# Selective-scan mixer: three of a state's four turned tiles weighed by ScalarE and summed in DRAM, one by VectorE

## The chip, the cores and the metric

One core of one Trainium2 chip runs the kernel. The metric is the device time of one execution in microseconds, the median over the runs; each run is one launch of the whole program.

## What is computed

The reference is a two-layer model on an input of 8 sequences of 512 tokens with 256 features. The change touches only the first mixer, a selective state-space scan with 512 channels and 16 states per channel, on each of the 8 sequences:

```
xz = x @ W_in;  xs, res = split(xz)
u = silu(grouped_conv4(xs) + conv_b)
dbc = u @ W_x                       # 64 columns for delta, 16 for B, 16 for C
delta = clip(softplus(dbc[:64] @ W_dt + b_dt), 0.001, 0.1)
dA = exp(delta * A)                 # per channel and state
h_t = dA_t * h_{t-1} + delta_t * u_t * B_t
y_t = sum over the 16 states n of h_t[n] * C_t[n]
out = (y + u * D) * silu(res) @ W_out
```

After it come an attention layer, a mixture of experts with routing, a second mixer and a second mixture of experts. All is float32.

## The kernel before

The program runs five stages one after the other; each ends with a barrier over the five engines. The first, StageA, is this mixer. Everything below is in it.

**States as the unit of work.** The work is cut into K = 128 states: 8 sequences (blocks b) times 16 states n, k = 16 b + n. A state has two halves f = 0 and 1 of 256 channels each (two groups of 128 partitions, 512 tokens along the free axis). For one half:

- `fill` (L695): GpSimd multiplies du = delta * u by the row of B of that state, which SP has broadcast from DRAM to all partitions (L383, 256 KB), into a buffer h (L702). There are eight such buffers, four states' worth.
- `drive` (L577): ScalarE writes the decays exp(delta * A) with two activations (L584) into PSUM, banks 0 and 1 for one half, 2 and 3 for the other.
- `recur` (L648): VectorE runs the recurrence over the tokens, in place in h (L652).
- `turn` (L465 on TensorE, L588 on ScalarE, L654 on VectorE): the product with C is a weight per token, so TensorE first turns h from channels-by-tokens into four tiles i = 0 to 3 of 128 tokens by 512 channels, four transposes each (L472). Bank 4 takes tiles 0 and 1, one after the other; VectorE multiplies each by its column of C and adds it to the running sum `acc` in SBUF (L665, or L662 without the add for the first state of a block). Bank 5 takes tiles 2 and 3; ScalarE multiplies each by its column into `pr` in SBUF (L599; for the first state straight into `acc`).
- `add` (L705): GpSimd issues a DMA that adds the two tiles of `pr` (512 KB) onto the half of `acc` that belongs to tiles 2 and 3 (L713). It waits for the DMA of the state before. There are two `pr` buffers.

**The order.** `order` (L318) writes one list of steps, and every engine walks it and does what concerns it, in that order. The list runs over half-states h = 2k + f. Within one, lines L333 to L344 decide:

```python
out += [step for step in pieces if step[0] in self.TAKE]
if k in range(K):
    out.append(("recur", k, f))
if f and k - 2 in range(K):
    out.append(("add", k - 2))
if k - 1 in range(K):
    out.append(("turn", k - 1, f))
if k + 1 in range(1, K):
    out.append(("drive", k + 1, f))
if k + 2 in range(1, K):
    out.append(("fill", k + 2, f))
out += [step for step in pieces if step[0] not in self.TAKE]
```

So a turn follows its scan by a state, an add by two, and a fill comes two states before its scan.

**The pieces.** What prepares the next block (layer norm, transposes, the projections and the convolution on TensorE, their evictions by ScalarE, the two Silus with their table loads, softplus, clip, du) and what finishes the block before (`back`, the sums turned back; `gate` on VectorE; `proj`, the output projection; `back_to_x`) is cut into pieces. Two tables written by hand, PREP (L295) and END (L309), deal them out over the 32 half-states of a block. PREP's numbers count from the start of the block before, END's from the start of the block after. `bank` (L278) hands PSUM banks 6 and 7 to the pieces in turn. The pieces of ScalarE that come closest together are `silu` (L551: a table load, two activations of 2048 columns, a table load) at half-state 16, `mixed` at 18, four `stepped` at 20 to 23, and `soft` (L573) at 23.

**Queues.** SP issues the broadcasts of B, each once GpSimd is through with the buffer two states back. GpSimd issues the adds between its own multiplications. `back` waits for all adds of its block (L478).

Of the kernel before, what the change touches and what calls it, by code (L numbers as in the profile page):

```python
# [219 lines left out]
class StageA:  # L220
# [6 lines left out]
    def __init__(self, m):  # L227
        self.m = m
        ar = Arena(m.Z, m.LO, m.HI)
# [8 lines left out]
        self.nb = ar.take([4])  # L238
        self.n_tm = ar.take([4, 256])
        self.n_fm = ar.take([2, 515])  # L240
        self.dbc = ar.take([512], parts=96)
        self.ct = [ar.take([4, 32]) for _ in range(2)]
# [11 lines left out]
        self.turn_d, self.turn_a = m.banks[4], m.banks[5]  # L254
        self.scr = [m.nc.dram_tensor(f"rows_b{q}", [16, 512], F32, kind="Internal").ap() for q in range(2)]
        self.steps = self.order()
        first = {}
        for what, *at in self.steps:
# [8 lines left out]
            "d_win", "d_conv", "d_rest", "d_scr", "pads", "neg", "win_t", "tapped", "taps", "moments", "rstd", "nb", "n_tm", "made0", "made1", "gate", "u",  # L267
            "raw", "delta", "du", "hin", "decay", "scan", "turn_d", "turn_a", "ysum", "yprod", "yadd", "yp")}

# [19 lines left out]
    def over(self, *step):  # L289
# [5 lines left out]
    PREP = (  # L295
        (-11, ("stats",)), (-10, ("rstd",), ("minus",)), (-9, ("norm",)), (-6, ("flip", 0)),
        (-5, ("flipped", 0), ("flip", 1)), (-4, ("flipped", 1)), (-3, ("conv", 0, 0), ("conv", 0, 1)),
        (-2, ("conv", 0, 2), ("conv", 0, 3)), (-1, ("conv", 0, 4)), (0, ("conv", 0, 5), ("conv", 0, 6)),
        (1, ("conv", 0, 7), ("conv", 1, 0)), (2, ("conved", 0), ("conv", 1, 1)), (3, ("conv", 1, 2), ("conv", 1, 3)),
        (4, ("conv", 1, 4), ("conv", 1, 5)), (5, ("conv", 1, 6)), (6, ("conv", 1, 7), ("conv", 2, 0)),  # L300
        (7, ("conved", 1), ("conv", 2, 1), ("conv", 2, 2)), (8, ("conv", 2, 3)), (9, ("conv", 2, 4), ("conv", 2, 5)),
        (10, ("conv", 2, 6), ("conv", 2, 7)), (11, ("conved", 2), ("conv", 3, 0)), (12, ("conv", 3, 1), ("conv", 3, 2)),
        (13, ("conv", 3, 3), ("conv", 3, 4)), (14, ("conv", 3, 5)), (15, ("conv", 3, 6), ("conv", 3, 7)),
        (16, ("conved", 3), ("silu",)), (17, ("mix",)), (18, ("mixed",)), (19, ("side",), ("step", 0)),
        (20, ("spill",), ("sided",), ("stepped", 0), ("step", 1), ("lift", 0)),
        (21, ("stepped", 1), ("step", 2), ("lifted", 0), ("lift", 1)), (22, ("stepped", 2), ("step", 3), ("lifted", 1)),
        (23, ("stepped", 3), ("soft",)), (24, ("clip",), ("lift", 2)), (25, ("du",), ("lifted", 2)), (26, ("lift", 3)),
        (27, ("lifted", 3)))
    END = (  # L309
        (7, ("back", 0)), (8, ("gate", 0), ("back", 1)), (9, ("gate", 1), ("back", 2)), (10, ("gate", 2), ("back", 3)),  # L310
        (11, ("gate", 3)), (12, ("proj", 0, 0), ("proj", 0, 1), ("proj", 0, 2)),
        (13, ("proj", 0, 3), ("proj", 0, 4), ("proj", 0, 5)), (14, ("proj", 0, 6), ("proj", 0, 7)), (15, ("back_to_x", 0)),
        (16, ("proj", 1, 0), ("proj", 1, 1), ("proj", 1, 2)), (17, ("proj", 1, 3), ("proj", 1, 4), ("proj", 1, 5)),
        (18, ("proj", 1, 6), ("proj", 1, 7)), (19, ("back_to_x", 1)))

    FIRST, LAST = -3, 16
# [37 lines left out]
    def sp(self, e):  # L354
# [29 lines left out]

        self.walk(spill=spill, fill=fill)

    def pe(self, e):
# [77 lines left out]
        def turn(k, f):  # L465
            for (o, i, free, made) in ((self.turn_d, f, "ysum", "turn_d"), (self.turn_a, 2 + f, "yprod", "turn_a")):
                if f == 0:
                    e.wait_ge(s["scan"], 2 * k + 2)
                if k or f:
                    e.wait_ge(s[free], 2 * k + f)  # L470
                for c in range(4):
                    ins = e.transpose(o[:, c * 128:(c + 1) * 128], self.h(k, c // 2)[:, c % 2, i * 128:(i + 1) * 128], ident)  # L472
                ins.then_inc(s[made], 1)

        def back(b, c):
            if c == 0:
                e.wait_ge(s["ysum"], 32 * (b + 1))
                e.wait_ge(s["yadd"], 16 * 15 * (b + 1))  # L478
            o = bank("back", b, c)
            for i in range(4):  # L480
                ins = e.transpose(o[:, i * 128:(i + 1) * 128], self.acc[b % 2][:, i, c * 128:(c + 1) * 128], ident)
            ins.then_inc(s["made1"], 1)
# [15 lines left out]
    def act(self, e):  # L498
# [26 lines left out]
        def norm(b):  # L525
            s6, mv, r = self.sb
            e.wait_ge(s["nb"], b + 1)
            if b:
                e.wait_ge(*self.made("flip", b - 1, 1))
            for i in range(4):  # L530
# [69 lines left out]

# [4 lines left out]
    def dve(self, e):  # L605
# [31 lines left out]
        def sided(b):  # L637
            o, over, before = self.bank("side", b)
            e.wait_ge(*self.made("side", b))
            if b >= 2:  # L640
                e.wait_ge(s["yprod"], 32 * (b - 1))
            e.tensor_copy(self.ct[b % 2].rearrange(FLAT), o[:, 0:128]).then_inc(*over)
# [10 lines left out]

        def turn(k, f):  # L654
            b, n = divmod(k, 16)
            e.wait_ge(s["turn_d"], 2 * k + f + 1)
            o, c = self.acc[b % 2][:, f, :], self.ct[b % 2][:, f, 16 + n:17 + n]
            if n == 0:
                e.wait_ge(*self.over("side", b))
                if b >= 2:  # L660
                    e.wait_ge(*self.made("back", b - 2, 3))
                e.tensor_scalar(o, self.turn_d, c, None, ALU.mult).then_inc(s["ysum"], 1)  # L662
            else:
                e.wait_ge(s["ysum"], 2 * (k - 1) + f + 1)
                e.scalar_tensor_tensor(o, self.turn_d, c, o, ALU.mult, ALU.add).then_inc(s["ysum"], 1)  # L665

# [19 lines left out]
    def pool(self, e):  # L686
# [8 lines left out]
        def fill(k, f):  # L695
            b, n = divmod(k, 16)
            if k % 16 == 0:
                e.wait_ge(s["du"], b + 1)
            e.wait_ge(self.d_B[k % 2], 16 * (k // 2 + 1))
            if k >= 4:  # L700
                e.wait_ge(s["turn_a"], 2 * (k - 4) + 2)
# [12 lines left out]

# [1802 lines left out]
```

## Time and profile before

| | us |
|---|---|
| median of 3 runs | 3337.27 |
| lowest and highest | 3325.84 and 3342.91 |
| the profiled execution, its own time | 3336.9 |
| its span, first to last instruction | 3335.1 |
| mean granted TensorE clock over it | 0.927 of full speed |
| first scan starts | 99.3 |
| last scan starts | 1001.1 |

The profile is of one execution. Engines: PE is TensorE, DVE VectorE, ACT ScalarE, POOL GpSimd. Busy time is that of instructions; an instruction that issues a DMA is not counted as busy. The idle time of a group is that of its engine just before it, with what ended it behind the arrow. Two instructions that follow each other on one engine can overlap by some 0.1 us in the trace, so the cost of one in a full stretch is best read from the distance of starts.

### The profile page before, as it was taken

To read this page: it belongs to the slowest core of one execution; us is meant where nothing else is said; L and a number is where in the kernel's file an instruction comes from. 1 tells how busy PE (TensorE), PEld (TensorE's weight loads), DVE (VectorE), ACT (ScalarE), POOL (GpSimd) and SP (SyncE) were. 2 spreads that over 40 slices of the span, in tenths; PEclk is the share of its full clock that TensorE was granted. 3 is DMA by queue.
4 is the path that set the end of the run, shared out by engine and by line. 5 is a ranking of instruction groups with operands and counts; after the bars stand their busy time and mean duration, and the time that the engine had idled before them with its cause. 6 is when DMAs were issued, how large, how long until landed. Compare 5 with 4: busy or idle time off the path is not lost.

```text
span 3335.1 us, 40739 instructions
## 1 busy us (share of the span) xinstructions
PE 2797.5 (84%) x13719; PEld 1686.9 (51%) x13782; DVE 2184.5 (65%) x3943; ACT 1569.1 (47%) x2311; POOL 1043.2 (31%) x705
## 2 busy tenths in 40 slices
PE   7778887787764699999966999948988887999999
PEld 3444454454452355555543666624444444666666
DVE  0698898899893676777532222226777775777776
ACT  2677667766761245555541111137777782111111
POOL 0887787788871111112102111012111100010000
PEclk9898998999866899999988999978999998999999
DMA  3354444454552744555323000010000002000000
GB/s 108 80 112 107 105 104 103 96 113 103 111 110 61 105 70 83 86 89 95 63 104 81 26 23 23 17 49 13 7 7 7 7 1 58 7 7 13 7 7 13
DMA packets 120347, 198.60 MB, mean 60 GB/s; under 512 B 15728, under 2 KB 78064, under 8 KB 118992
## 3 DMA queue, kind: packets, MB, share of 16 engines
q1 hardware_dynamic: 97504, 124.24, 16.5%
q0 software_dynamic: 22640, 71.75, 10.9%
q8 instruction: 116, 1.90, 0.2%
q14 instruction: 87, 0.71, 0.1%
HBM read 107.12 MB, written 25.91 MB: 40 GB/s over the span
## 4 chain that ended last, share of the span: by engine, by line
PE 51%; ACT 5%; DVE 5%; issue 4%; DMA 2%; POOL 0%; SPq 0%; ACTq 0%; DVEq 0%; POOLq 0%
PE PS L1517 7%; PE PS L2222 7%; PE PS L2240 6%; PE PS L1539 4%; PE PS L1810 3%; PE PS L1182 2%; PE PS L1859 2%; ACT Z L1963 2%; PE PS L1817 2%; PE PS L1161 2%; PE PS L1164 2%; PE PS L1109 1%; PE PS L1139 1%; PE PS L1877 1%; PE PS L1208 1%
## 5 line engine op out<-in xcount | busy, mean ns | idle before, releaser
L702 POOL TENSOR_TENSOR Z<-Z 128x1024 f32<-128x1024 f32 x256 | 652.7, 2661 | 109.5 <-PE PS L472 109.3
L652 DVE TENSOR_TENSOR_SCAN Z<-PS,Z 128x1024 f32<-128x1024 f32 x256 | 583.3, 2279 | 7.7 <-ACT PS L584 7.7
L472 PE MATMUL PS<-Z 128*128 128x128 f32 x2048 | 313.9, 301 | 139.8 <-DVE Z L665 131.9
L472 PEld LDWEIGHTS PS<-Z 128*128 128x128 f32 x2048 | 259.1, 156 | 288.4 <-DVE Z L652 145.2
L584 ACT ACTIVATE PS<-Z 128x511 f32<-128x511 f32 x512 | 332.2, 683 | 91.9 <-DVE Z L652 91.0
L1275 ACT ACTIVATE Z<-PS 128x512 f32<-128x512 f32 x320 | 189.1, 597 | 262.5 <-PE PS L1164 259.0
L2222 PE MATMUL PS<-Z 128*128 128x512 f32 x576 | 273.8, 600 | 17.5 <-DVE Z L2355 17.5
L440 PE MATMUL PS<-Z 128*128 128x512 f32 x512 | 254.6, 614 | 36.3 <-ACT Z L519 35.6
L2273 ACT ACTIVATE Z<-PS 128x512 f32<-128x512 f32 x144 | 86.0, 597 | 416.8 <-PE PS L2222 416.8
L1370 DVE TENSOR_REDUCE Z<-PS 128x1 f32<-128x512 f32 (+2 forms) x384 | 182.7, 508 | 114.6 <-PE PS L1140 109.9
L1963 ACT ACTIVATE Z<-Z 128x2048 f32<-128x2048 f32 x128 | 252.7, 2000 | 10.3 <-PE PS L1859 8.5
L599 ACT ACTIVATE Z<-PS,Z 128x512 f32<-128x512 f32 x256 | 175.7, 686 | 163.1 <-PE PS L472 133.6
L1517 PE MATMUL PS<-Z 128*128 x560 | 248.4, 597 | 0.8 <-issue 0.6
L2240 PE MATMUL PS<-Z 128*128 128x256 f32 x1024 | 242.4, 380 | 0.0
L2067 DVE TENSOR_SCALAR Z<-Z 128x512 f32<-128x512 f32 x512 | 235.0, 529 | 5.1 <-ACT Z L1963 5.1
L2240 PEld LDWEIGHTS PS<-Z 128*128 128x128 f32 x1024 | 193.4, 190 | 78.1 <-issue 54.1
L2370 DVE SCALAR_TENSOR_TENSOR Z<-PS,Z 128x256 f32<-128x256 f32 x512 | 214.0, 476 | 9.9 <-PE PS L2240 9.9
L665 DVE SCALAR_TENSOR_TENSOR Z<-PS,Z 128x512 f32<-128x512 f32 x240 | 175.2, 730 | 55.7 <-PE PS L472 55.5
L2106 POOL TENSOR_TENSOR Z<-Z 128x512 f32<-128x512 f32 x32 | 44.4, 1416 | 433.4 <-ACT Z L1895 433.4
L2355 DVE TENSOR_TENSOR Z<-Z,PS 128x512 f32<-128x512 f32 x144 | 98.2, 687 | 122.7 <-ACT Z L2273 122.7
L1645 DVE TENSOR_TENSOR Z<-Z,PS 128x512 f32<-128x512 f32 x70 | 48.2, 689 | 197.9 <-PE PS L1517 197.9
L1416 POOL TENSOR_TENSOR Z<-Z 128x512 f32<-128x512 f32 x32 | 36.9, 1154 | 414.2 <-ACT Z L1242 414.2
(278 smaller groups left out, 5021.6 us busy)
## 6 DMA issues: line engine op xcount, KB each, us to landing
Z<-Z POOLq DMA_DIRECT2D x120, 512.0 KB, 4.6
Z<-rows_b SPq DMA_DIRECT2D x128, 256.0 KB, 3.1
Z<-scr SPq DMA_DIRECT2D x256, 128.0 KB, 5.7
scr<-Z SPq DMA_DIRECT2D x32, 384.0 KB
Z<-in_L_ffn_expert_wv SPq DMA_DIRECT2D x4, 2048.0 KB, 14.6
rows_y<-Z SPq DMA_DIRECT2D x35, 128.0 KB, 1.7
Z<-in_L_attn_x SPq DMA_DIRECT2D x8, 512.0 KB, 8.9
rows_n<-Z SPq DMA_DIRECT2D x8, 512.0 KB, 2.9
```

Of the source, the lines that this page charges most:

```text
L440: ins = e.matmul(self.bank("conv", b, c)[0], self.conv[:, w, k, c * 128:(c + 1) * 128], self.n_fm[:, k, w:w + 512], start=i == 0, stop=i == 7)
L472: ins = e.transpose(o[:, c * 128:(c + 1) * 128], self.h(k, c // 2)[:, c % 2, i * 128:(i + 1) * 128], ident)
L584: ins = e.activation(self.aa[f][:, c, 1:512], self.de[b % 2][:, 2 * f + c, 1:512], ACT.Exp, scale=self.An[:, q:q + 1])
L652: e.tensor_tensor_scan(h, a, h, 0.0, ALU.mult, ALU.add).then_inc(s["scan"], 1)
L702: e.tensor_tensor(self.h(k, f), self.du[b % 2][:, 2 * f:2 * f + 2, :], b3(self.Bs[k % 2], 1, [128, 2, 512]), ALU.mult).then_inc(s["hin"], 1)
L1275: e.activation(self.pt[n % 8], self.tbank[n % 2], ACT.Exp).then_inc(s["exp"], 1)
L1517: ins = e.matmul(ub[n], self.hs[c % 2][:, k, :], self.wv[:, bass.ds(expert[c] * 4096 + (2048 * k + 512 * n), 512)], start=k == 0, stop=k == 1)
L1963: e.activation(self.e[u % 10], self.An, ACT.Exp, scale=self.dl[b % 2][:, j, i:i + 1]).then_inc(s["grow"], 1)
L2067: ins = e.tensor_scalar(o, o, 1e-6, self.bc[b % 2][:, 4 * j + i, q:q + 1], ALU.max, ALU.mult)
L2222: ins = e.matmul(self.up[n % 2], w, self.nf[b % 2][:, k, :], start=k == 0, stop=k == 1)
L2240: ins = e.matmul(o[:, j * 256:(j + 1) * 256], self.hd[n % 4][:, c], self.w2[:, x - 1, :], start=True, stop=True)
L2370: ins = e.scalar_tensor_tensor(xx, o[:, j * 256:(j + 1) * 256], self.cw[b % 2][:, t, x - 1:x], xx, ALU.mult, ALU.add)
```

## The change

The four tiles of a state are shared otherwise. TensorE uses banks 4 and 5 in turn for tiles 0 to 3. VectorE weighs tile 0 alone, once per state in half-state f = 0, and keeps its sum in SBUF, now 512 columns wide. ScalarE weighs tiles 1 to 3: one in half-state 0 and two in half-state 1, always into `pr`, which has three tiles (768 KB) and three buffers. The add moves to half-state 0, covers three tiles and goes to a DRAM tensor `sums`, two of them in turn; the first add of a block is a plain store. The last block's sum alone stays in SBUF, in a buffer of u. Every add waits for the one before. A new step `recall` loads a block's sums back (SP's queue, 768 KB) into `rest`, which shares its space with the normalised input `n_tm` and with `dbc`; so `norm` and `mixed` wait for a `back`, and `recall` for the readers of both. The tables PREP and END are dealt anew: the pieces move by up to three half-states; `silu`, `mixed`, `side` and `soft` keep theirs.

```diff
-        self.acc = [ar.take([4, 512]) for _ in range(2)]
-        self.pr = [ar.take([2, 512]) for _ in range(2)]
+        self.acc = [ar.take([512]) for _ in range(2)]
+        self.pr = [ar.take([3, 512]) for _ in range(3)]
+        self.sums = [m.nc.dram_tensor(f"sums{q}", [128, 3, 512], F32, kind="Internal").ap() for q in range(2)]
...
+    def sum(self, b):
+
+        return self.sums[b % 2] if b + 1 < NB else self.u[NB % 3][:, 0:3, :]
...
     END = (
-        (7, ("back", 0)), (8, ("gate", 0), ("back", 1)), (9, ("gate", 1), ("back", 2)), (10, ("gate", 2), ("back", 3)),
-        (11, ("gate", 3)), (12, ("proj", 0, 0), ("proj", 0, 1), ("proj", 0, 2)),
...
+        (6, ("recall",)), (8, ("back", 0)), (9, ("gate", 0), ("back", 1), ("gate", 1), ("back", 2)),
+        (10, ("gate", 2), ("back", 3)), (11, ("gate", 3), ("proj", 0, 0), ("proj", 0, 1), ("proj", 0, 2)),
...
-            if f and k - 2 in range(K):
+            if not f and k - 2 in range(K):
                 out.append(("add", k - 2))
...
+        def recall(b):
+            if b + 1 == NB:
+                return
+            e.wait_ge(s["d_sum"], 16 * 16 * (b + 1))
+            if b + 2 < NB:
+                e.wait_ge(*self.made("flip", b + 2, 1))
+            e.wait_ge(*self.made("step", b + 1, 3))
+            e.wait_ge(*self.made("side", b + 1))
+            e.wait_ge(s["d_scr"], 16 * (b + 2))
+            e.dma_start(self.rest, self.sum(b)).then_inc(s["d_recall"], 16)
...
         def turn(k, f):
-            for (o, i, free, made) in ((self.turn_d, f, "ysum", "turn_d"), (self.turn_a, 2 + f, "yprod", "turn_a")):
-                if f == 0:
+            for i in (2 * f, 2 * f + 1):
+                if i == 0:
                     e.wait_ge(s["scan"], 2 * k + 2)
-                if k or f:
-                    e.wait_ge(s[free], 2 * k + f)
+                    if k:
+                        e.wait_ge(s["yprod"], 3 * k - 1)
+                elif i == 2:
+                    e.wait_ge(s["ysum"], k + 1)
+                elif k or i == 3:
+                    e.wait_ge(s["yprod"], 3 * k if i == 1 else 3 * k + 1)
                 for c in range(4):
...
+            for i in (2, 3) if f else (1,):
+                e.wait_ge(s["turn"], 4 * k + i + 1)
+                if i == 1 and k >= 3:
+                    e.wait_ge(s["d_sum"], 16 * (k - 2))
+                e.activation(self.pr[k % 3][:, i - 1, :], self.turned[i % 2], ACT.Copy,
+                             scale=self.ct[b % 2][:, i, 16 + n:17 + n]).then_inc(s["yprod"], 1)
...
         def turn(k, f):
+            if f:
+                return
             b, n = divmod(k, 16)
...
         def add(k):
             b, n = divmod(k, 16)
+            e.wait_ge(s["yprod"], 3 * k + 3)
+            if k:
+                e.wait_ge(s["d_sum"], 16 * k)
             if n == 0:
-                return
-            e.wait_ge(s["yprod"], 2 * k + 2)
-            if n > 1:
-                e.wait_ge(s["yadd"], 16 * (15 * b + n - 1))
-            o = self.acc[b % 2][:, 2:4, :]
-            e.dma_start(o, self.pr[k % 2], accum_op=ALU.add).then_inc(s["yadd"], 16)
+                if b >= 2:
+                    e.wait_ge(s["d_recall"], 16 * (b - 1))
+                if b + 1 == NB:
+                    e.wait_ge(s["yp"], 4 * (NB - 2))
+                e.dma_start(self.sum(b), self.pr[k % 3]).then_inc(s["d_sum"], 16)
+            else:
+                e.dma_start(self.sum(b), self.pr[k % 3], accum_op=ALU.add).then_inc(s["d_sum"], 16)
```

## Rows read from the trace of the kernel before

**Rows 1.** Busy time in windows: block 0, blocks 1 to 6, block 7; us.
```profile
core 0: us, PE busy (x) PEld busy (x) DVE busy (x) ACT busy (x) POOL busy (x), PEclk, DMA share, GB/s
99.30:206.80 107.50, 85.60 (x358) 46.87 (x358) 93.18 (x74) 80.12 (x122) 96.22 (x49) 0.93 0.46 103
206.80:902.80 696.00, 554.43 (x2454) 334.15 (x2454) 619.96 (x503) 476.27 (x725) 555.16 (x289) 0.92 0.48 105
902.80:1004.00 101.20, 66.70 (x304) 54.11 (x304) 97.77 (x75) 64.22 (x97) 79.83 (x44) 0.63 0.54 116
```

**Rows 2.** VectorE in order of time from 551 us: start, duration, line.
```profile
551.81 2.28 DVE L652 TENSOR_TENSOR_SCAN Z<-PS,Z 128x1024 f32<-128x1024 f32 x1
554.01 0.73 DVE L665 SCALAR_TENSOR_TENSOR Z<-PS,Z 128x512 f32<-128x512 f32 x1
554.65 2.28 DVE L652 TENSOR_TENSOR_SCAN Z<-PS,Z 128x1024 f32<-128x1024 f32 x1
...
564.79 0.75 DVE L662 TENSOR_SCALAR Z<-PS,Z 128x512 f32<-128x512 f32 x1 [2.18 <-PE PS L472]
```

**Rows 3.** Groups of instructions, blocks 1 to 6 (96 states).
```profile
L702 POOL TENSOR_TENSOR Z<-Z 128x1024 f32<-128x1024 f32 x193 | 493.2, 2655 | 94.5 <-PE PS L472 94.5
L652 DVE TENSOR_TENSOR_SCAN Z<-PS,Z 128x1024 f32<-128x1024 f32 x193 | 439.8, 2279 | 0.0
L584 ACT ACTIVATE PS<-Z 128x511 f32<-128x511 f32 x385 | 249.9, 683 | 76.2 <-DVE Z L652 75.6
...
L665 DVE SCALAR_TENSOR_TENSOR Z<-PS,Z 128x512 f32<-128x512 f32 x181 | 132.2, 730 | 46.4 <-PE PS L472 46.3
L599 ACT ACTIVATE Z<-PS,Z 128x512 f32<-128x512 f32 x192 | 131.7, 686 | 119.0 <-PE PS L472 95.9 <-DMA Z<-Z 22.9
```

**Rows 4.** ScalarE in order of time from 616 us.
```profile
616.79 1.28 ACT L554 ACT_TABLE_LOAD   x1
...
623.11 0.69 ACT L599 ACTIVATE Z<-PS,Z 128x512 f32<-128x512 f32 x1
...
627.19 0.68 ACT L599 ACTIVATE Z<-PS,Z 128x512 f32<-128x512 f32 x1
628.50 1.30 ACT L584 ACTIVATE PS<-Z 128x511 f32<-128x511 f32 x2 [0.63 <-DVE Z L652]
```

**Rows 5.** GpSimd in order of time from 660 us.
```profile
660.36 5.00 POOL L702 TENSOR_TENSOR Z<-Z 128x1024 f32<-128x1024 f32 x2
665.00 1.20 POOL L713 DMA_DIRECT2D Z<-Z  x1
...
681.48 1.32 POOL L713 DMA_DIRECT2D Z<-Z  x1
```

**Rows 6.** The source view of L713, the add: issue to landing.
```profile
L713 POOL DMA_DIRECT2D Z<-Z x120: 852/878/1360, 122.3 to 1009.5; - x120
...
DMA to landing us min/median/max: 4.5/4.6/7.5
```

**Rows 7.** DMA queues, 606 to 614 us: one add, one broadcast.
```profile
q0 software_dynamic: 144, 0.52, 34.6%
q1 hardware_dynamic: 144, 0.26, 8.8%
...
Z<-rows_b SPq DMA_DIRECT2D x1, 256.0 KB, 3.1
```

**Rows 8.** DMA issues, whole span: 512 KB stored to DRAM by SP.
```profile
rows_n<-Z SPq DMA_DIRECT2D x8, 512.0 KB, 2.9
```

**Rows 9.** Windows of the scan (L652) alone: one stretch of six states.
```profile
655.70:691.70 36.00, 27.31 (x12) 0.95 0.50 110
```

**Rows 10.** The stage's end in order of time, all engines.
```profile
1009.53 0.86 POOL L713 DMA_DIRECT2D Z<-Z  x1 [4.42 <-DMA Z<-Z]
...
1014.18 1.09 PE L481 MATMUL PS<-Z 128*128 128x128 f32 x4 [6.07 <-issue]
```

More of the change, by code:

```diff
@@ L238, in __init__ @@
         self.nb = ar.take([4])
-        self.n_tm = ar.take([4, 256])
+        self.rest = ar.take([3, 512])
+        self.n_tm = self.rest[:, 0:2, :].rearrange("p a (b c) -> p (a b) c", c=256)
+        self.dbc = self.rest[0:96, 2, :]
         self.n_fm = ar.take([2, 515])
-        self.dbc = ar.take([512], parts=96)
         self.ct = [ar.take([4, 32]) for _ in range(2)]
@@ L267, in __init__ @@
             "d_win", "d_conv", "d_rest", "d_scr", "pads", "neg", "win_t", "tapped", "taps", "moments", "rstd", "nb", "n_tm", "made0", "made1", "gate", "u",
-            "raw", "delta", "du", "hin", "decay", "scan", "turn_d", "turn_a", "ysum", "yprod", "yadd", "yp")}
+            "raw", "delta", "du", "hin", "decay", "scan", "turn", "ysum", "yprod", "d_sum", "d_recall", "yp")}
+    def sum(self, b):
+        return self.sums[b % 2] if b + 1 < NB else self.u[NB % 3][:, 0:3, :]
     def h(self, k, f):
@@ L295 @@
     PREP = (
[L296 to L300, printed above, removed]
@@ L301 @@
-        (7, ("conved", 1), ("conv", 2, 1), ("conv", 2, 2)), (8, ("conv", 2, 3)), (9, ("conv", 2, 4), ("conv", 2, 5)),
-        (10, ("conv", 2, 6), ("conv", 2, 7)), (11, ("conved", 2), ("conv", 3, 0)), (12, ("conv", 3, 1), ("conv", 3, 2)),
-        (13, ("conv", 3, 3), ("conv", 3, 4)), (14, ("conv", 3, 5)), (15, ("conv", 3, 6), ("conv", 3, 7)),
+        (-10, ("stats",), ("rstd",)), (-8, ("minus",)), (-7, ("norm",)), (-5, ("flip", 0), ("flipped", 0)),
+        (-4, ("flip", 1), ("flipped", 1)), (-3, ("conv", 0, 0), ("conv", 0, 1), ("conv", 0, 2), ("conv", 0, 3)),
@@ L304 @@
+        (13, ("conv", 3, 4)), (14, ("conv", 3, 5)), (15, ("conv", 3, 6), ("conv", 3, 7)),
         (16, ("conved", 3), ("silu",)), (17, ("mix",)), (18, ("mixed",)), (19, ("side",), ("step", 0)),
         (20, ("spill",), ("sided",), ("stepped", 0), ("step", 1), ("lift", 0)),
-        (21, ("stepped", 1), ("step", 2), ("lifted", 0), ("lift", 1)), (22, ("stepped", 2), ("step", 3), ("lifted", 1)),
-        (23, ("stepped", 3), ("soft",)), (24, ("clip",), ("lift", 2)), (25, ("du",), ("lifted", 2)), (26, ("lift", 3)),
@@ L308 @@
-        (27, ("lifted", 3)))
+        (21, ("stepped", 1), ("step", 2), ("lifted", 0)),
+        (22, ("lift", 1), ("stepped", 2), ("step", 3), ("lifted", 1)), (23, ("stepped", 3), ("soft",)),
+        (24, ("clip",), ("lift", 2)), (25, ("du",), ("lifted", 2), ("lift", 3)), (27, ("lifted", 3)))
     END = (
-        (7, ("back", 0)), (8, ("gate", 0), ("back", 1)), (9, ("gate", 1), ("back", 2)), (10, ("gate", 2), ("back", 3)),
-        (11, ("gate", 3)), (12, ("proj", 0, 0), ("proj", 0, 1), ("proj", 0, 2)),
@@ L318, in order @@
+        (13, ("proj", 0, 3), ("proj", 0, 4), ("proj", 0, 5)), (14, ("proj", 0, 6)), (15, ("proj", 0, 7)),
+        (16, ("back_to_x", 0)), (17, ("proj", 1, 0), ("proj", 1, 1), ("proj", 1, 2), ("proj", 1, 3), ("proj", 1, 4)),
+        (18, ("proj", 1, 5)), (19, ("proj", 1, 6), ("proj", 1, 7)), (20, ("back_to_x", 1)))
+    FIRST, LAST = -3, 17
     def order(self):
@@ L383, in fill @@
             e.dma_start(self.Bs[k % 2], self.scr[b % 2][n:n + 1, :].partition_broadcast(128)).then_inc(self.d_B[k % 2], 16)
-        self.walk(spill=spill, fill=fill)
+        def recall(b):
[8 more added lines that the diff above has]
+            e.dma_start(self.rest, self.sum(b)).then_inc(s["d_recall"], 16)
+        self.walk(spill=spill, fill=fill, recall=recall)
     def pe(self, e):
@@ L465, in turn @@
         def turn(k, f):
-            for (o, i, free, made) in ((self.turn_d, f, "ysum", "turn_d"), (self.turn_a, 2 + f, "yprod", "turn_a")):
-                if f == 0:
+            for i in (2 * f, 2 * f + 1):
+                if i == 0:
                     e.wait_ge(s["scan"], 2 * k + 2)
-                if k or f:
-                    e.wait_ge(s[free], 2 * k + f)
+                    if k:
[4 more added lines that the diff above has]
+                    e.wait_ge(s["yprod"], 3 * k if i == 1 else 3 * k + 1)
                 for c in range(4):
-                    ins = e.transpose(o[:, c * 128:(c + 1) * 128], self.h(k, c // 2)[:, c % 2, i * 128:(i + 1) * 128], ident)
-                ins.then_inc(s[made], 1)
+                    ins = e.transpose(self.turned[i % 2][:, c * 128:(c + 1) * 128],
+                                      self.h(k, c // 2)[:, c % 2, i * 128:(i + 1) * 128], ident)
+                ins.then_inc(s["turn"], 1)
         def back(b, c):
             if c == 0:
-                e.wait_ge(s["ysum"], 32 * (b + 1))
-                e.wait_ge(s["yadd"], 16 * 15 * (b + 1))
+                e.wait_ge(s["ysum"], 16 * (b + 1))
+                if b + 1 < NB:
+                    e.wait_ge(s["d_recall"], 16 * (b + 1))
+                else:
+                    e.wait_ge(s["d_sum"], 16 * 16 * NB)
             o = bank("back", b, c)
+            rest = self.rest if b + 1 < NB else self.sum(b)
             for i in range(4):
-                ins = e.transpose(o[:, i * 128:(i + 1) * 128], self.acc[b % 2][:, i, c * 128:(c + 1) * 128], ident)
+                y = rest[:, i - 1, c * 128:(c + 1) * 128] if i else self.acc[b % 2][:, c * 128:(c + 1) * 128]
+                ins = e.transpose(o[:, i * 128:(i + 1) * 128], y, ident)
             ins.then_inc(s["made1"], 1)
@@ L529, in norm @@
                 e.wait_ge(*self.made("flip", b - 1, 1))
+            if b >= 3:
+                e.wait_ge(*self.made("back", b - 3, 3))
             for i in range(4):
@@ L565, in mixed @@
                 e.wait_ge(*self.made("side", b - 1))
+            if b >= 2:
+                e.wait_ge(*self.made("back", b - 2, 3))
             evac(self.dbc, "mix", b)
@@ L640, in sided @@
             if b >= 2:
-                e.wait_ge(s["yprod"], 32 * (b - 1))
+                e.wait_ge(s["yprod"], 48 * (b - 1))
+                e.wait_ge(s["ysum"], 16 * (b - 1))
             e.tensor_copy(self.ct[b % 2].rearrange(FLAT), o[:, 0:128]).then_inc(*over)
@@ L661, in turn @@
                     e.wait_ge(*self.made("back", b - 2, 3))
-                e.tensor_scalar(o, self.turn_d, c, None, ALU.mult).then_inc(s["ysum"], 1)
+                e.tensor_scalar(o, y, c, None, ALU.mult).then_inc(s["ysum"], 1)
             else:
-                e.wait_ge(s["ysum"], 2 * (k - 1) + f + 1)
-                e.scalar_tensor_tensor(o, self.turn_d, c, o, ALU.mult, ALU.add).then_inc(s["ysum"], 1)
+                e.wait_ge(s["ysum"], k)
+                e.scalar_tensor_tensor(o, y, c, o, ALU.mult, ALU.add).then_inc(s["ysum"], 1)
         def gate(b, c):
@@ L700, in fill @@
             if k >= 4:
-                e.wait_ge(s["turn_a"], 2 * (k - 4) + 2)
+                e.wait_ge(s["turn"], 4 * (k - 3))
             e.tensor_tensor(self.h(k, f), self.du[b % 2][:, 2 * f:2 * f + 2, :],
```

27 lines of the change are left out of this document (10 added, 17 removed).

## Prediction, made before the changed kernel was run

> **What bounds the kernel now.** The windows come first. Of the 3335.1 us span, the scan mixer's states take 107.5 us for block 0, 696.0 for blocks 1 to 6 and 101.2 for block 7; VectorE is busy for 93.2, 620.0 and 97.8 of these, 89% of blocks 1 to 6, and no other engine has more (GpSimd 80%, without the issuing of its adds; TensorE 80%; ScalarE 68%) [rows 1]. That is 6.72, 7.25 and 6.33 us a state. VectorE in order of time shows the floor: scan, eviction and next scan start 2.20 and 0.64 us apart, so 2.84 a half and 5.68 a state when nothing is missing [rows 2]. The remaining 1.57 us a state of blocks 1 to 6 are pieces of other work and waits. The groups name the waits: 46.4 us before the evictions of L665, all on TensorE's transposes, as in the 2.18 us at 564.79 [rows 2, 3]. So VectorE is the bound, with bursts in which ScalarE or TensorE is late.
>
> The others are not far. GpSimd, when it catches up, issues an add at 665.00 and the third after it at 681.48: 5.49 us a state for two multiplications and an add, its own floor [rows 5]. ScalarE has 476.3 us over 96 states, 4.96 a state [rows 1].
>
> **VectorE, the gain.** One of two evictions per state goes: 128 times 0.64 us [rows 2] is 81.9 us. The floor becomes 5.04 us a state. What covered the rest of the stage must be no slower: GpSimd's 5.49 plus du already is above that floor, but under the mean after the gain, 7.25 - 0.64 = 6.61.
>
> **ScalarE, part given back.** It gets a third eviction per state, 0.69 us each [rows 3], so 4.96 + 0.69 = 5.65 us a state with its pieces, below 6.61. Mostly this lies beside the scans: ScalarE waits 119.0 us for transposes and 76.2 for scans in blocks 1 to 6 [rows 3]. It lies on the path where ScalarE has no gap: from 616.79, the first table load, it works without a wait to 627.87, and VectorE's evictions and scans queue behind it [rows 4]. There everything behind is late by each added eviction. With the evictions of `stepped` and `soft` behind that stretch the full zone is about half-states 16 to 25, five states: 5 x 0.69 = 3.4 us a block, in the seven blocks that prepare another one: +24 us. Bounds: 0 (the added eviction always finds a gap) and 0.69 x 128 = 88.
>
> **The add, now through DRAM: the term that decides.** An add lands 4.5 to 4.6 us after its issue [rows 6], and the next may not be issued before. Today that is below any state's 5.68. Of it, the data take the queue's share of 16 engines, 34.6% of 8 us, 2.77 us for 512 KB, while a plain broadcast of 256 KB takes 8.8%, 0.70 us: per byte an accumulating transfer costs twice a plain one [rows 7]. For 768 KB the data are 4.15 us, and the landing 4.5 - 2.77 + 4.15 = 5.9 us, if DRAM answers like SBUF. No row shows an accumulation in DRAM. From the nearest: the broadcast reads DRAM and lands after 3.1 us, 2.4 over its data [rows 7]; a 512 KB store lands after 2.9 us [rows 8], 1.5 over the 1.4 that its data take at the broadcast's rate; so reading DRAM first may add up to 0.9. I take 5.9 + 0.5 = 6.4, and 6.5 a state with the wait between. The lower end is 3.9, the data at a plain rate (2.1 us) with both sources read at once; the upper one 4.6 scaled whole by 1.5, plus 0.9, is 7.8.
>
> At 6.5 the chain fits under the mean of 6.61, but not in the stretches without pieces. From 655.7 us six states (12 scans) took 36.0 us, 6.00 each [rows 9]; less 0.64 that is 5.36, and the chain falls behind by 6 x 1.14 = 6.8 us. The fills that stand behind an add in GpSimd's order are two states early: two states of 5.04 less GpSimd's own 5.49 leave about 5 us of cushion. The loss is some 2 us a block, +12 for six. Block 0: 107.5 - 10.2 + 3.4 = 100.7 by the engines, 104.0 by the chain: +3. Block 7 adds in SBUF, 5.9 and 0.1 of wait, 96.0 against 101.2 - 10.2 = 91.0: +5.
>
> The Trainium skill (DMA: Bandwidth & Descriptors, the section on the anatomy of one DMA on the GpSimd path) gives for any such DMA about 2.0 us plus its bytes at 436 GB/s. That would be an estimated 3.8 us for 768 KB, and no loss to the chain at all. For 512 KB it gives 3.2 us, where this trace has 4.6 [rows 6]; the rule does not count what accumulating costs, so the row goes first. The same section says that the confirmation of a write is heaviest when the target is HBM, which speaks against the change; the trace has only plain stores to set beside it.
>
> **GpSimd's issue.** 0.88 us an add [rows 6] stays, of which 0.5 shows; a 16th add a block: 8 x 0.5 = 4 us beside other work, 0. The add's move by half a state puts it before both fills; it waits for the third eviction of two states back and for the add before, and both fills queue behind it, with the cushion named. Bounds as for the chain.
>
> **Three buffers.** ScalarE's 22.9 us of waits for a landing [rows 3] should go: it now waits for the add three states back. VectorE did not stand on these, so 0.
>
> **recall and the shared space.** Eight blocks less one, 768 KB each on SP's queue, after the block's last add has landed; SP's next broadcast stands behind it, which GpSimd needs about a state later. Covered by that state, 0; without the cover about 2 us a block. The waits of `norm` and `mixed` on a `back` are for pieces over ten half-states old: 0. The load's data, 2.1 us at the broadcast's rate [rows 7], share the engines with one add: +1 a block at most, within the range.
>
> **The transposes.** As many as before; bank 4 now waits for ScalarE's tile 2 of the state before, half a state old: 0. **The pieces dealt anew**: their instructions are the same; I give 0, with 3 us a block either way (two waits as the one at 564.79), 20 in all.
>
> **The tail.** After the last scan the last add lands 4.65 us after 1009.53 [rows 10]; at 768 KB 1.4 later, and ScalarE has one more eviction in the row: +2.5.
>
> **Sum.** -81.9 + 24 + 12 + 3 + 5 + 2.5 = -35.4. Against the profiled execution's 3336.9 us, which is 0.4 under the median, that is 3301.5; I say 3302 us, 1.1% less. About 0.5%, 17 us, is what a measurement of this kernel can tell from no change.
>
> **Rivals.**
> - Full relief. The add is short (up to 6.0 us a state) and ScalarE's third eviction finds gaps: -81.9 + 2.5 gives 3257. For it: ScalarE's 195 us of waits. Against it: the doubled cost per byte, and GpSimd's floor of 5.49. This is also what the skill's formula would give.
> - Slower: the chain of adds in DRAM sets the pace of every state in blocks 0 to 6. They take 803.5 us now, 7.17 a state; above that landing-plus-wait the change loses. At 7.5 + 0.1: 112 x 7.6 = 851, +48, less 5 in block 7 and plus 2.5: 3382. At the upper end, 7.8 + 0.1: 885, +79, 3416. For it: no cushion helps against a mean, and GpSimd's fills stand behind the wait. Against it: DRAM would have to add over 1.2 us to the 5.9, and the rows bear 0.9.
> - ScalarE becomes the pacemaker: its chain of transposes, evictions and decays has no gap in the short state, so each state gets back the 0.69 us it lost on VectorE: 88 against 82, within 10 us of 3337. For it: 2.6 us of decays and 2.1 of evictions a state fill 4.7 of a floor of 5.04.
>
> **Chances.** Forecast 0.42, full relief 0.13, the DRAM chain 0.25, ScalarE 0.20. The forecast's own range is 3285 to 3320. The range to the rivals: 3257 below; above, 3385, which holds the DRAM chain up to a landing of 7.5. Faster takes the forecast less a little, and full relief: 0.52. Same, ScalarE and edges: 0.20. Slower: 0.28.
>
> **What would show it.** Right: one L665-kind eviction a state and the distance of two scans without one 2.20; landing of the adds 6.2 to 6.7; GpSimd waiting for the DMA of the add before in the stretches without pieces; a longer run of ScalarE without a gap at `silu`; blocks 1 to 6 near 111 us each. Wrong: landings over 7.1 with GpSimd waiting in every state, or ScalarE with hardly a wait and VectorE waiting for it in each state, or blocks near 106.

## The result and the profile after

The changed kernel takes 3374.38 us (median of 4 runs, 3368.1 to 3376.51), the one before beside it 3338.05. The ratio is 1.0122, with a 95% interval of 1.0098 to 1.0147: slower by 1.2%, where 1.1% faster was forecast. The profiled execution has a span of 3373.7 us, 38.6 more than before.

The windows of block 0, blocks 1 to 6 and block 7, from first scan to first scan (columns: stretch and length, then busy time and count of TensorE, weight loads, VectorE, ScalarE, GpSimd; TensorE's granted clock; DMA share; GB/s):

```profile
97.70:207.20 109.50, 89.69 (x359) 50.74 (x360) 85.63 (x58) 83.78 (x133) 91.97 (x47) 0.89 0.64 131
207.20:920.20 713.00, 560.86 (x2460) 340.79 (x2459) 569.01 (x406) 523.75 (x824) 559.13 (x295) 0.92 0.74 148
920.20:1030.50 110.30, 67.68 (x303) 52.28 (x302) 88.41 (x58) 72.08 (x112) 86.48 (x47) 0.62 0.70 154
```

Set beside [rows 1], block 0 takes 109.5 us for 107.5, blocks 1 to 6 713.0 for 696.0, block 7 110.3 for 101.2. VectorE lost 51 us of work in blocks 1 to 6 and is busy for 80% instead of 89%. DMA went from 0.48 to 0.74 of its engines' time. TensorE's clock is nearly the same.

The groups of blocks 1 to 6 (count, busy us, mean ns, then the idle time before them and what ended it):

```profile
L732 POOL TENSOR_TENSOR Z<-Z 128x1024 f32<-128x1024 f32 x193 | 482.1, 2680 | 0.1
L680 DVE TENSOR_TENSOR_SCAN Z<-PS,Z 128x1024 f32<-128x1024 f32 x193 | 436.9, 2278 | 64.2 <-POOL Z L732 54.2 <-ACT PS L615 9.9
...
L625 ACT ACTIVATE Z<-PS,Z 128x512 f32<-128x512 f32 x290 | 188.1, 685 | 109.8 <-DMA sums<-Z 74.9 <-PE PS L493 34.7
L747 POOL DMA_DIRECT2D sums<-Z x90 | 81.0, 900 | 144.4 <-DMA sums<-Z 84.9 <-PE PS L493 43.4 <-ACT Z L625 16.1
...
L695 DVE SCALAR_TENSOR_TENSOR Z<-PS,Z 128x512 f32<-128x512 f32 x90 | 66.3, 737 | 49.1 <-PE PS L493 48.1
...
L674 DVE TENSOR_SCALAR Z<-Z 128x2048 f32<-128x2048 f32 x6 | 24.6, 4099 | 12.3 <-ACT Z L606 12.3
```

VectorE has half the evictions (L695, [rows 3]), and for it a new wait: 64.2 us before scans, 54.2 of them on GpSimd's multiplication, where there was none [rows 3]. GpSimd waits 144.4 us before issuing adds, ScalarE 74.9 us for a buffer that an add still reads. The clip (L674) takes 4.10 us in the mean of these blocks. The source view of the add and GpSimd in order of time, four adds in a row:

```profile
L747 POOL DMA_DIRECT2D sums<-Z x105: 871/878/1217, 119.7 to 938.2; - x105
...
  DMA sums<-Z: 101.1, 58
...
DMA to landing us min/median/max: 5.7/6.6/8.6
```

```profile
641.07 0.88 POOL L747 DMA_DIRECT2D sums<-Z  x1 [2.54 <-DMA sums<-Z]
641.65 5.00 POOL L732 TENSOR_TENSOR Z<-Z 128x1024 f32<-128x1024 f32 x2
648.11 0.88 POOL L747 DMA_DIRECT2D sums<-Z  x1 [1.46 <-PE PS L493]
...
655.10 0.87 POOL L747 DMA_DIRECT2D sums<-Z  x1 [1.41 <-PE PS L493]
...
661.98 0.89 POOL L747 DMA_DIRECT2D sums<-Z  x1 [1.31 <-DMA sums<-Z]
```

GpSimd's two multiplications end at 646.65, and the next add goes out at 648.11. The distances are 7.04, 6.99 and 6.88 us: a landing of 6.53, 6.47 and 6.37 us, and 0.51 us until the next issue. The view puts some of these waits down to TensorE, which had long been done; the distance, the same whatever is named, says that it is the landing.

It is so through the whole stage, in long states too. Call the distance from one add's issue to the next a link. Of the stage's 127 links, 117 end 0.51 to 0.55 us after the landing; in blocks 1 to 6 it is 89 of 96, with a landing of 6.77 us in the mean, and these 89 links take 7.29 us. The exception comes once a block (and one other time in these six), behind the multiplication that makes `du` (L723):

```profile
667.20 4.83 POOL L723 TENSOR_TENSOR Z<-Z 128x2048 f32<-128x2048 f32 x1
671.67 1.20 POOL L747 DMA_DIRECT2D sums<-Z  x1
```

The add before, issued at 661.98, had landed at 668.42, but GpSimd issues the next one only after its fills and `du`, 3.2 us later. Such a link takes 9.7 us. Fifteen of 7.29 and one of 9.7 are 119 us, and a block takes 118.8: the chain of adds sets the mean pace.

The issues of the adds by destination (count, KB, us to landing), whole span:

```profile
sums<-Z POOLq DMA_DIRECT2D x112, 768.0 KB, 6.6
...
Z<-Z POOLq DMA_DIRECT2D x16, 768.0 KB, 5.8
```

An add into DRAM lands after 6.6 us in the median, the same 768 KB in SBUF (block 7) after 5.8. At the stage's end the backlog is seen:

```profile
1041.11 0.86 POOL L747 DMA_DIRECT2D Z<-Z  x1 [5.40 <-DMA Z<-Z]
1047.35 0.86 POOL L747 DMA_DIRECT2D Z<-Z  x1 [5.38 <-DMA Z<-Z]
...
1053.15 1.09 PE L508 MATMUL PS<-Z 128*128 128x128 f32 x4 [16.91 <-issue]
```

The last scan starts at 1027.67 and is over by 1030; three more adds then go out one after the other, and TensorE turns the first sum back at 1053.15. From last scan to first turning back are 25.5 us; before, 13.05 [rows 10, with the last scan at 1001.13]. The whole difference: start -1.6, block 0 +2.0, blocks 1 to 6 +17.0, block 7 +9.1, tail +12.4, together +38.9 of the 38.6.

### The profile page after: what moved, and what is told of

Same layout as the page of the kernel before. It is cut to its first block, busy times and chain, and to the rows that moved or that the text cites. A ratio compares the mean times of both kernels' runs of the same rounds, so it can differ in the third digit from the quotient of the medians.

```text
span 3373.7 us, 40404 instructions
## 1 busy us (share of the span) xinstructions
PE 2812.6 (83%) x13719; PEld 1696.0 (50%) x13782; DVE 2114.5 (63%) x3815; ACT 1629.7 (48%) x2439; POOL 1050.2 (31%) x713
## 4 chain that ended last, share of the span: by engine, by line
PE 51%; ACT 5%; DVE 5%; issue 3%; DMA 2%; POOL 0%; SPq 0%; ACTq 0%; DVEq 0%; POOLq 0%
PE PS L1551 7%; PE PS L2256 7%; PE PS L2274 6%; PE PS L1573 4%; PE PS L1844 3%; PE PS L1216 2%; PE PS L1893 2%; ACT Z L1997 2%; PE PS L1195 2%; PE PS L1198 2%; PE PS L1851 2%; PE PS L1143 2%; PE PS L1173 2%; PE PS L1911 1%; PE PS L1242 1%
## 5 line engine op out<-in xcount | busy, mean ns | idle before, releaser
L732 POOL TENSOR_TENSOR Z<-Z 128x1024 f32<-128x1024 f32 x256 | 637.5, 2668 | 0.2
L493 PE MATMUL PS<-Z 128*128 128x128 f32 x2048 | 331.4, 307 | 161.6 <-DVE Z L695 75.0
L493 PEld LDWEIGHTS PS<-Z 128*128 128x128 f32 x2048 | 261.5, 157 | 313.3 <-DVE Z L695 102.4
L625 ACT ACTIVATE Z<-PS,Z 128x512 f32<-128x512 f32 x384 | 249.5, 685 | 156.0 <-DMA sums<-Z 91.7
L2274 PEld LDWEIGHTS PS<-Z 128*128 128x128 f32 x1024 | 193.4, 190 | 78.0 <-issue 54.0
L1551 PEld LDWEIGHTS PS<-Z 128*128 128x128 f32 x560 | 104.5, 192 | 119.5 <-issue 119.5
```

Of the source, the lines that this page charges most:

```text
L493: ins = e.transpose(self.turned[i % 2][:, c * 128:(c + 1) * 128], self.h(k, c // 2)[:, c % 2, i * 128:(i + 1) * 128], ident)
L625: e.activation(self.pr[k % 3][:, i - 1, :], self.turned[i % 2], ACT.Copy, scale=self.ct[b % 2][:, i, 16 + n:17 + n]).then_inc(s["yprod"], 1)
L1551: ins = e.matmul(ub[n], self.hs[c % 2][:, k, :], self.wv[:, bass.ds(expert[c] * 4096 + (2048 * k + 512 * n), 512)], start=k == 0, stop=k == 1)
L2274: ins = e.matmul(o[:, j * 256:(j + 1) * 256], self.hd[n % 4][:, c], self.w2[:, x - 1, :], start=True, stop=True)
```

## The experiments

Three theories. **1:** the chain of landings of the adds sets the pace. **2:** ScalarE's third eviction does. **3:** the new deal of the pieces costs the time. Each ratio is to the kernel before, run beside; its median differs by up to 12 us between the groups of runs (3326.6 to 3338.1), so small differences of two runs are to be read from the ratios.

**two_chains.**

```diff
+        self.sums = [[m.nc.dram_tensor(f"sums{q}{c}", [128, 3, 512], ...) for c in range(2)] for q in range(2)]
...
+            if k >= 2:
+                e.wait_ge(*self.landed(k - 2))
```

> The changed kernel, but in blocks 0 to 6 the adds of even and odd states go to two DRAM tensors, so an add waits for the landing of the add two states back instead of one. The sums of the odd states are left out of the result (only the first tensor is loaded back), block 7 keeps its single chain in SBUF. Theory 1, the chain of landings sets the pace (6.5 us landing and 0.45 to the next issue make the 7.0 us a state seen): GpSimd no longer waits for a landing, blocks 1 to 6 fall from 118.8 us to 112 or less, block 0 by 6, block 7 and the tail stay; about 3326 us. Theory 2, ScalarE's third eviction sets the pace: no change, 3370 +- 8. Theory 3, the new deal of the pieces does: no change either, 3370.

Measured 3301.16 us, ratio to the kernel before 0.9897 (0.9875 to 0.9919): 73 us below the changed kernel, and 25 below the 3326 that theory 1 had expected. Its windows and groups for blocks 1 to 6, and block 7:

```profile
208.10:856.40 648.30, 536.90 (x2454) 331.02 (x2452) 563.89 (x407) 524.57 (x822) 553.27 (x294) 0.94 0.80 163
856.40:959.00 102.60, 64.28 (x307) 50.58 (x308) 88.15 (x59) 73.49 (x114) 82.48 (x45) 0.72 0.74 163
```

```profile
L685 DVE TENSOR_TENSOR_SCAN Z<-PS,Z 128x1024 f32<-128x1024 f32 x194 | 436.0, 2275 | 10.1 <-ACT PS L620 10.1
...
L755 POOL DMA_DIRECT2D sums<-Z x84 | 83.2, 990 | 70.3 <-PE PS L498 45.0 <-ACT Z L630 24.3 <-issue 1.0
```

Blocks 1 to 6 take 648.3 instead of 713.0 us, though each add now lands later: 7.9 us in the median, with two in flight. GpSimd's wait before an add is halved and no landing is in it, and no scan waits for GpSimd. States without pieces now take 5.0 us, the floor of 5.04 that was forecast; in the changed kernel they took 7.0. The DMA engines' throughput is not what held it, since their share rises from 0.74 to 0.80. Block 7, whose chain is still single but now starts without a backlog, falls from 110.3 to 102.6 us; the tail stays, 25.6 us from the last scan to the first turning back. Theory 1 holds, 2 and 3 fall as the main cause.

**two_tiles.**

```diff
-                e.dma_start(self.sum(b), self.pr[k % 3], accum_op=ALU.add)
+                e.dma_start(self.sum(b)[:, 0:2, :], self.pr[k % 3][:, 0:2, :], accum_op=ALU.add)
```

> The changed kernel, but each DMA stores, adds and loads back two of ScalarE's three tiles (512 KB instead of 768 KB); ScalarE still makes all three, and the third one's sum is left out of the result. Theory 1: the landing falls by the data of a third, 1.4 us, to 5.2, the chain to 5.7 us a state; blocks 1 to 6 near 110 us, block 7 near 102, the tail back to 16 us or less; about 3308 us. Theory 2 (ScalarE) and theory 3 (the tables): ScalarE and the tables are untouched, so 3370 +- 8.

Measured 3308.59 us, 0.9939 (0.9915 to 0.9964). The adds' issues, in DRAM and, in block 7, in SBUF:

```profile
sums<-Z POOLq DMA_DIRECT2D x112, 512.0 KB, 5.8
...
Z<-Z POOLq DMA_DIRECT2D x16, 512.0 KB, 5.0
```

With an unchanged order of waits, fewer bytes alone bring back the time: 662.3 us for blocks 1 to 6. The chain still has no slack in 79 of their 96 links, of 6.6 us in the mean, and yet states 0 to 3 run at 5.0 to 5.4 us: a link longer than the short states costs little, 14 us against two_chains. Sixteen links of 6.6 us are 106 us, below the 108 us of a block in two_chains. The landing in DRAM is 5.8 us for 512 KB where the kernel before has 4.6 in SBUF [rows 6] and this one, in block 7, 5.0. So the landing is about 1 us longer for DRAM, and 0.8 us longer for each 256 KB, less than the 1.4 expected.

**old_tables.**

```diff
-    PREP, END, LAST of the changed kernel
+    PREP, END, LAST of the kernel before, with (6, ("recall",))
```

> The changed kernel with the pieces dealt out as in the kernel before (its PREP, END and LAST; recall stays at half-state 6). Theory 3, the new deal costs the time: 3345 or less. Theory 1 and 2: the chain or ScalarE sets the pace whatever the deal, 3374 +- 12.

Measured 3381.48 us, 1.0137 (1.0115 to 1.0160). **new_tables**, the counterpart on the kernel before:

```diff
-    PREP, END, LAST of the kernel before
+    PREP, END, LAST of the changed kernel, without recall
```

> The kernel before with the new PREP, END and LAST, without recall; nothing else changed. Theory 3: slower by 20 us or more than before, 3360. Theory 1 and 2: within 12 us of 3338.

Measured 3312.01 us, 0.9929 (0.9907 to 0.9951): 24 us faster. Blocks 1 to 6:

```profile
204.10:875.70 671.60, 564.63 (x2453) 339.34 (x2452) 609.02 (x503) 478.01 (x725) 553.35 (x288) 0.91 0.49 108
```

671.6 us against 696.0. Theory 3 is wrong in sign, and theories 1 and 2 had expected within 12 us: none had this. The new deal is worth 24 us with short adds. Where the chain sets the pace at most 7 of them are left (3374 against 3381), and the intervals of those two ratios overlap, so it may be none.

**narrow_one_chain.**

```diff
+                w = 64 if i == 3 and k >= 3 else 512
+                e.activation(self.pr[k % 3][:, i - 1, 0:w], self.turned[i % 2][:, 0:w], ACT.Copy, ...)
```

> The changed kernel with its single chain and full 768 KB adds, but ScalarE evicts only 64 of the 512 columns of tile 3 from the fourth state on, so tile 3's sums are wrong. ScalarE is relieved of most of its third eviction, the chain is not. Theory 1, the chain sets the pace: 3374 -10 to +4. Theory 2, ScalarE does: 3340 or less.

Measured 3384.43 us, 1.0176 (1.0154 to 1.0198): no faster at all, and 6 us above the upper end that theory 1 had given. An eviction of 64 columns still takes 0.31 us against 0.68 for 512, so this relieves ScalarE of 0.37 us a state. Blocks 1 to 6, and the line of the add's source view that says what ended its waits:

```profile
206.80:929.70 722.90, 563.61 (x2460) 340.56 (x2459) 573.06 (x407) 488.57 (x824) 558.75 (x295) 0.91 0.74 146
```

```profile
  DMA sums<-Z: 112.7, 65
```

ScalarE lost 35 us of work in blocks 1 to 6 (488.6 for 523.8), and the blocks took 10 us more. Again 89 of the 96 links have no slack; they take 7.40 us in the mean instead of 7.29, which makes the 10 us. Theory 2 falls in the changed kernel.

**chains_full**, nothing left out:

```diff
+            e.dma_start(self.de[b % 2][:, 0:3, :], self.sum(b, 1)).then_inc(s["d_recall1"], 16)
...
+                for part in (rest, odd):
+                    ins = e.matmul(o[:, i * 128:(i + 1) * 128], part[:, i - 1, c * 128:(c + 1) * 128], ident,
+                                   start=part is rest, stop=part is odd)
```

> The changed kernel with two chains of adds and nothing left out: even and odd states' sums are both loaded back (the odd ones into the free delta buffer) and TensorE adds the two while it turns them back; block 7 has two chains in SBUF as well. Theory 1: blocks 1 to 6 stay at 109 us as with two chains, block 7 goes from 102.6 to about 97, the tail from the last scan to the first turn back from 25 us to about 14: 3301 - 6 - 8 + 2 for the second loads, about 3289 us, faster than both kernels. If the second load or the longer landings of two adds in flight cost more than they free, 3305 or more.

Measured 3326.18 us, 0.9994 (0.9980 to 1.0008), 37 above what was expected. The transposes of `acc` that wait for the loads (L519):

```profile
L519 PE MATMUL PS<-Z x32: 300/330/475, 228.2 to 1014.9; 128*128 128x128 f32 x32
...
  DMA Z<-sums: 17.5, 7
```

State 4 of blocks 1 to 7 takes 14.1 to 19.7 us, against 10.9 with one load (two_chains), since TensorE stands on the second load with the scans' transposes queued behind it: in all seven the first transpose of `acc` starts 0.2 to 0.3 us after that load has landed. The expectation's second branch came true, 3305 or more with costly loads: 686.3 us for blocks 1 to 6, and 102.8 for block 7, with none of its gain. The tail alone came as in the first branch, at 13.1 us.

**narrow**, the kernel of chains_full with ScalarE relieved and two tiles in the DMAs:

```diff
+                w = 64 if i == 3 else 512
+                e.activation(self.pr[k % 3][:, i - 1, 0:w], self.turned[i % 2][:, 0:w], ACT.Copy, ...)
```

> The kernel with two chains complete, but ScalarE evicts only 64 of the 512 columns of tile 3, whose sums are left out of the result (the DMAs move two tiles). It prices ScalarE's third eviction once the chain is gone. If ScalarE gives back what VectorE gained (6.5 us a block seen between the new deal alone, 112.7, and two chains, 109.0, against the 10.2 that VectorE saves): blocks fall to 104 us or less and the time by 30 us or more below the complete one. If the give-back is elsewhere (the clip that waits for GpSimd, TensorE's order): within 8 us.

Measured 3293.56 us, 0.9898 (0.9878 to 0.9919), 33 us under chains_full, but not as expected: a block takes 111 us, not 104. Most of the 33 is state 4, now 12.9 us, because the two loads move a third less; that is mixed into this run and not ScalarE's price. What can be put down to ScalarE are the states with its bursts: state 9, with the Silus, 11.4 for 11.8 us, and state 12 10.9 for 11.3. That is 0.8 us a block for the 0.37 us a state by which ScalarE is relieved. For the whole eviction of 0.69 us an estimate by proportion is 1.5 us a block, not 3.4.

**clip_alone**, against chains_full:

```diff
+            if n == 14 and f == 0 and b + 1 < NB:
+                e.wait_ge(s["delta"], b + 2)
```

> The kernel with two chains complete, but once a block GpSimd does not start its multiplication for state 14 before VectorE's clip of the next block is done. With two chains that clip takes 3.8 us where it takes 1.2 to 1.7 in the kernels with VectorE at two tiles. If the clip is stretched because GpSimd is multiplying beside it: it takes 1.3 us and 2 us a block, some 15 us, are won. If GpSimd's later start makes scans wait instead: no gain or slower.

Measured 3334.89 us, 1.0022 (1.0005 to 1.0039), 9 us above chains_full. The clip (min, median and max in ns):

```profile
L690 DVE TENSOR_SCALAR Z<-Z x8: 1228/1228/1231, 89.7 to 880.0; 128x2048 f32<-128x2048 f32 x8
```

The clip is 1.23 us in every block, so GpSimd's multiplication beside it stretches it, and state 12 falls from 11.3 to 8.7. But states 3 and 4 take 7 and over 17 us. Both branches came true, and the second is the larger.

**late**, against chains_full, with this and the pieces behind it moved in END:

```diff
-        (6, ("recall",)), (8, ("back", 0)), (9, ("gate", 0), ("back", 1), ("gate", 1), ("back", 2)),
+        (6, ("recall",)), (10, ("back", 0)), (11, ("gate", 0), ("back", 1)), (12, ("gate", 1), ("back", 2)),
```

> Two chains complete, with the turning back of the sums two half-states later and one gate per half-state. In the complete version before it state 4 of each block took 14 to 20 us, against 10.9 with one load, because TensorE waited for the second load of the sums. If that wait is all that it lost: blocks 1 to 6 at 109 us or less, block 7 at 98, about 3288 us, faster than both kernels. If the two loads and longer landings cost elsewhere: 3315 or more.

Measured 3294.14 us, 0.9898 (0.9874 to 0.9923), with the full result, 6 above the 3288 expected. Windows of blocks 1 to 6 and of block 7, TensorE's first turning back after the last scan, and the adds' landings:

```profile
203.60:863.80 660.20, 561.27 (x2670) 357.24 (x2668) 563.56 (x407) 525.55 (x822) 552.88 (x294) 0.94 0.80 167
863.80:960.90 97.10, 65.25 (x343) 52.91 (x344) 87.61 (x59) 73.82 (x114) 83.07 (x47) 0.76 0.86 191
```

```profile
971.15 0.45 PE L519 MATMUL PS<-Z 128*128 128x128 f32 x1 [6.97 <-DMA Z<-Z]
```

```profile
DMA to landing us min/median/max: 5.7/8.5/10.3
```

The wait for the second load was most of it: 660.2 us for blocks 1 to 6 and 97.1 for block 7. The tail from the last scan at 958.08 is 13.1 us, as before the change. This is the fastest complete kernel here, though its lead over new_tables (0.9929) is within the two intervals.

**late_clip.** The diffs of late and clip_alone together.

> The same, with GpSimd's multiplication for state 14 held until VectorE's clip is done. With the loads covered, the 2.6 us a block that the clip lost (state 12 at 8.7 instead of 11.3 us) should stay won: 15 us below the run without it, about 3273 us. If GpSimd's late start makes VectorE wait at states 3 and 4, as it seemed before (7.0 instead of 5.0 us), nothing is won.

Measured 3301.2 us, 0.9916 (0.9895 to 0.9938): nothing won. The median is 7 us above that of late; the intervals overlap, but in the profiled executions blocks 1 to 6 take 672.7 against 660.2 us. ScalarE's waits for GpSimd's adds show where (the line of the add's source view on who waited for it):

```profile
  ACT Z L641: 41.0, 22
```

41.0 us, against 8.2 in late. State 12 keeps its 8.7 us, but state 3 takes 6.2 to 8.1 and state 4 6.8 to 9.8 us where late has 5.0 and 5.5. GpSimd held back for the clip sends its adds late into the stretch without pieces; ScalarE then has no free buffer. That these states' waits come from this alone was argued from the trace, not tried.

## Why the prediction was wrong

The mechanism that decides was named as a rival: the chain of adds in DRAM sets the pace of blocks 0 to 6, and the change loses when that pace is above 7.17 us a state. The forecast put it at 6.5, just under the mean of 6.61. It came out at 7.43 (713.0 us over 96 states).

**The add, now through DRAM.** The step that failed is "and 6.5 a state with the wait between". A link of the chain takes 7.29 us in the mean of blocks 1 to 6, and once a block 9.7 behind `du`. The landing was sized nearly right, 6.4 us against 6.6 in the median and 6.8 in the mean. The wait from a landing to the next issue is 0.52 us, not 0.1, and the 0.1 had been read from no row. It could have been: the last add of the kernel before, at 1009.53, waited for a DMA [rows 10], and the one ahead of it, issued at 1004.26, had landed at 1008.96, 0.57 us earlier. The link behind `du`, some 2.4 us longer, was not counted at all; by itself it takes a chain of 6.5 us from 104 us a block to an estimated 106, where the forecast's mean of 6.61 gives 105.8.

**The cushion.** That the chain may fall behind in the states without pieces and catch up in the long ones, for 2 us a block, was sound where its condition held: two_tiles, with links of 6.6 us, has blocks 1 to 6 at 14 us above two_chains, where +12 was forecast for 6.5. But a cushion only moves time from one state to another. In the changed kernel 16 links take 119 us, while the states without the chain take 108 a block (two_chains), so the cushion is used up and stays so. VectorE waited 54 us for GpSimd, and with the single chain taken away 65 us came back (713.0 to 648.3), against the 12 that the forecast had. Block 0, forecast at 104.0 us, took 109.5; two_chains has 106.7, so only some 3 us of it are the chain's.

**The tail.** +2.5 was forecast, +12.4 measured. Only the last add's own length was counted. The chain came to the end with three adds still to be issued one after the other.

**Block 7.** 96.0 us was forecast for a landing of 5.9 and 0.1 of wait. The landing was right in the median (5.8). The links took 6.2 to 7.1 us and the first 9.6, on top of the backlog from block 6: 110.3.

**VectorE, the gain.** The floor of 5.04 is right: two_chains runs at 5.0. But -0.64 us is not had in every state. Between new_tables and two_chains, with the same deal and neither held by a landing, blocks 1 to 6 differ by 23 us (671.6 and 648.3), where 96 x 0.64 = 61 was counted. States 4 and 7 did not shrink and state 9 grew by 0.7; state 12 grew from 7.9 to 11.3 and state 14 from 6.1 to 8.5. Why 14 grew no run shows. So a good part of what the engines were forecast to give came by luck: without the chain the forecast's terms put blocks 1 to 6 at 655 us, and two_chains has 648, but from a smaller gain of VectorE, a smaller price of ScalarE and the 24 us of the new deal, given as 0.

**ScalarE, part given back.** 3.4 us a block was too much where it can be seen, some 1.5 by the estimate from narrow. Of ScalarE's 119.0 us of waits before its evictions, all read as waits for transposes, 95.9 were that and 22.9 for landings [rows 3]. What took ScalarE's place is the clip: 1.21 us in the median of all eight before, 3.69 after, 3.83 in two_chains, and 1.23 as soon as GpSimd is kept still (clip_alone). In the kernel before, GpSimd was idle while the clip ran in seven of eight blocks, waiting to make du. The Trainium skill (SBUF — State Buffer, the section on who interferes with whom) says that a VectorE tensor_scalar in its two-port mode and GpSimd exclude each other for a whole instruction; the trace agrees: the clip that starts at 657.62 in the changed kernel ends at 661.76 instead of after 1.2 us, 1.1 us after GpSimd's two multiplications are over at 660.67, about its length when alone. It was held through the second of them too, which starts 0.4 us after the clip's own start; that is more than the section's sentence, that whoever issues first gets the ports for the whole instruction, lets one expect. That this clip runs in that mode is inferred from its wait.

**The pieces dealt anew.** Given as 0 with 20 us either way; it is -24 on the kernel before. Part of the change, it hides a larger loss: relative to new_tables the rest of the change costs 62 us.

**recall.** Given as 0, and with one load that holds: state 4 takes 10.9 us in two_chains as in new_tables, which has no load.

**The formula of the Trainium skill** (DMA: Bandwidth & Descriptors, the section on the anatomy of one DMA on the GpSimd path) for the DMA, an estimated 3.8 us for 768 KB, would have made the chain vanish; 6.6 in DRAM and 5.8 in SBUF were measured. The section's remark that the confirmation is heaviest for HBM fits the 0.8 to 1 us between them, but what part of it is reading and what confirming no run here separates.

Left open: why the adds of narrow_one_chain land later than those of the changed kernel, and how the 24 us of the new deal divide among the pieces. Nor was the change run with its 768 KB adds in SBUF, so how the loss divides between the third tile and DRAM is not shown. 768 KB in SBUF and 512 KB in DRAM both land after 5.8 us, and with the second two_tiles has no loss; that the first would have none either is argued from this, not tried.

## What to carry to other kernels

A chain in which each DMA waits for the one before is a bound of its own, with landing plus half a microsecond until the next issue as its link. Add what else stands before an issue on its engine, once a block here, and set the mean link against the mean state. Below it, a link longer than the short states costs little; above it, every state pays, and a backlog waits at the end. Accumulating into two places in turn lets each add wait for the one two states back, for the price of one more load and an addition that TensorE makes while transposing; here it paid only once the turning back came late enough for the second load (3326 against 3294 us). A change that bundles a new schedule with a new data path should be measured in its two halves: here one gained 24 us and the other lost 62.

## What had not been expected of the hardware

- An accumulation by DMA lands about 1 us later in DRAM than in SBUF: 5.8 against 4.6 to 5.0 us at 512 KB, 6.6 against 5.8 at 768 KB. From a landing to an issue on GpSimd that waited for it pass 0.51 to 0.55 us, 117 times in the changed kernel.
- With two accumulations in flight each lands after 7.9 us (two_chains) to 8.5 us (late), so two chains allow an add every 4.2 to 4.5 us (an estimate: half of landing plus 0.5) where one needs 7.3; and the broadcasts beside them land after 4.8 us instead of 3.1.
- A clip of 2048 columns by VectorE costs 1.2 us alone; beside GpSimd's multiplications 3.8 us in two_chains and 2.4 to 5.3 in the changed kernel.
